# A two-layer graph network: the second layer's Q projected first and gathered into a dense table, the feed-forward's first products issued one chunk ahead

## What is computed

```
q = (x @ Wq[l].T + bq[l]) * scaling;  k = x @ Wk[l].T;  v = x @ Wv[l].T
scores = sum over a head of q[tgt] * k[srcidx]          # per edge and head
w = softmax of scores over the edges of one target
agg = segment_sum(w * v[srcidx], tgt)
x = batchnorm(x + agg @ Wo[l].T + bo[l])
x = batchnorm(x + relu(x @ W1[l].T + b1[l]) @ W2[l].T + b2[l])
```

## Time and profile before

| | us |
|---|---|
| three runs | 3073.77, 3087.56, 3089.63 |
| median | 3087.56 |
| profiled execution, span from first to last instruction | 3095.6 |
| TensorE busy in it | 2657.9 (86%) |
| VectorE, ScalarE, GpSimd busy | 1629.2, 1321.1, 1115.8 |

### The profile page before, as it was taken

The page is one execution under the profiler, slowest core; times in us unless marked ns, Lnnn a source line. Parts: engine busy times, 40 slices in busy tenths (PEclk is TensorE's granted clock), DMA queues, the critical chain, the costliest instruction groups (busy, mean ns, idle before and its releaser), DMA issues.

```text
span 3095.6 us, 78344 instructions
## 1 busy us (share of the span) xinstructions
PE 2657.9 (86%) x32605; PEld 2143.5 (69%) x32605; DVE 1629.2 (53%) x3272; ACT 1321.1 (43%) x3690; POOL 1115.8 (36%) x1130
## 2 busy tenths in 40 slices
PE   5999997999999999758899788888888678599998
PEld 4877885777777777546488577777777465477777
DVE  5236785555555555456512355555554645656553
ACT  3324443555555555422232255555555322333432
POOL 0000002666666666400001267777777111222110
PEclk8999998999999999979999899999999889799998
DMA  5642003988899998641024489999999431122211
GB/s 195 228 175 107 31 28 140 317 313 316 309 331 322 317 325 297 222 121 41 14 97 154 160 321 354 352 349 347 350 347 352 126 113 57 38 89 92 69 59 58
DMA packets 231795, 621.75 MB, mean 201 GB/s; under 512 B 39008, under 2 KB 45792, under 8 KB 231427
## 3 DMA queue, kind: packets, MB, share of 16 engines
q0 software_dynamic: 137088, 466.78, 42.2%
q1 hardware_dynamic: 94339, 149.78, 14.6%
HBM read 538.80 MB, written 103.39 MB: 207 GB/s over the span
## 4 chain that ended last, share of the span: by engine, by line
PE 60%; DMA 16%; DVE 8%; POOL 7%; issue 6%; ACT 2%; SPq 0%; DVEq 0%; POOLq 0%; ACTq 0%
PE ps L1179 6%; DMA Y<-KVd,srcE 5%; PE ps L574 5%; PE ps L575 4%; PE ps L576 4%; DMA aggd<-stage,segs 4%; PE ps L1222 4%; PE ps L1209 4%; PE ps L774 3%; POOL Y L1096 3%; PE ps L942 2%; PE ps L944 2%; PE ps L943 2%; PE ps L1186 2%; PE ps L1872 2%
## 5 line engine op out<-in xcount | busy, mean ns | idle before, releaser
L1096 POOL DMA_INDIRECT Y<-KVd,srcE x449 | 430.2, 958 | 230.6 <-issue 115.8
L1370 ACT ACTIVATE stage<-ps,stage 128x128 f32<-128x128 f32 x832 | 294.8, 366 | 115.3 <-PE ps L1186 112.4
L1096 POOL DMA_INDIRECT WA<-KVd,srcE x186 | 179.3, 964 | 361.8 <-PE ps L576 268.1
L1351 ACT ACTIVATE work<-ps 128x512 f32<-128x512 f32 x309 | 179.8, 597 | 303.8 <-PE ps L1179 303.5
L1179 PE MATMUL ps<-ident,Y 128*128 128x128 f32 x1796 | 252.2, 280 | 32.2 <-DMA Y<-KVd,srcE 26.8
L1351 ACT ACTIVATE G<-ps 128x512 f32<-128x512 f32 x315 | 181.8, 597 | 223.5 <-PE ps L1179 223.1
L1277 DVE COPY G<-ps 128x512 f32<-128x512 f32 x208 | 143.8, 691 | 245.8 <-PE ps L1186 243.0
L574 PE MATMUL ps<-Wh,xs 128*128 128x512 f32 x600 | 238.7, 398 | 31.2 <-DVE xs L514 31.2
L1179 PEld LDWEIGHTS ps<-ident,Y 128*128 128x128 f32 x1796 | 199.2, 143 | 70.5 <-issue 49.3
L575 PE MATMUL ps<-Wl,xs 128*128 128x512 f32 x600 | 236.9, 395 | 0.0
L576 PE MATMUL ps<-Wh,xs 128*128 128x512 f32 x600 | 236.5, 394 | 0.0
(11 more groups left out here) (383 smaller groups left out, 6775.2 us busy)
## 6 DMA issues: line engine op xcount, KB each, us to landing
KVd<-stage SPq DMA_DIRECT2D x96, 256.0 KB, 2.0
aggd<-work SPq DMA_DIRECT2D x6, 2048.0 KB, 7.4
Qd<-stage SPq DMA_DIRECT2D x48, 256.0 KB, 2.0
G<-aggd SPq DMA_DIRECT2D x48, 256.0 KB, 2.7
Y<-KVd,srcE POOLq DMA_INDIRECT x449
Y<-in_x SPq DMA_DIRECT2D x4, 1536.0 KB, 14.7
G<-mixq SPq DMA_DIRECT2D x24, 256.0 KB
mixd<-rowsb SPq DMA_DIRECT2D x24, 256.0 KB
```

The source lines that it names most:

```text
L1096: pool.indirect_dma_start(out=kvs[a], out_offset=None, in_=KVd[l][:, :], in_offset=bass.IndirectOffsetOnAxis(ap=srcE[:, n:n + 1], axis=0)) ...
L1351: act.activation(kT[n % len(kT)], banks(l)[place_of(l, "k", n) % len(banks(l))][:, :], ACT.Copy).then_inc(out_a, 1)
L1370: last = act.activation(pT[g % len(pT)][:, P * i:P * (i + 1)], SC[g % 2][:, P * i:P * (i + 1)], ACT.Exp, bias=smin[:, t:t + 1], scale=-1.0 ...
```

## The change

- Layer 1's projections get an order of their own: Q of all 25 tiles first, then K and V.
- While K and V are made, GpSimd gathers the query slots of all 52 pairs from `Qd` into four zeroed buffers in turn (`BOUNCE`), and SP stores each, all 128 rows, to a new DRAM table `QS`.
- In layer 1's attention SP reads a pair's slots from `QS` into `qslot`; GpSimd no longer gathers them. GpSimd's nine early fetches under Q are gone: it begins when all tables and all slots are stored. `begin1` also waits for the slots on VectorE and ScalarE. Clearing `qslot` is left out in layer 1.
- In the feed-forward of both layers the first products of chunk c+1 are issued ahead of the second products of chunk c, in two banks of their own (4 and 5); W2's four blocks use banks 0 to 3. VectorE's order is as before.
- Some semaphores are merged (`pre_in`, `flag_made` into `pre_made`, `kv_in` renamed `ring_in`).

```diff
@@ attend_pool
-            kv_stored(pool, l)
             if l == 0:
+                kv_stored(pool)
                 pool.wait_ge(qkv_mm, QKV_E)
             else:
-                pool.wait_ge(w2_mm, WO)
+                tables_stored(pool, 1)
+                begin(pool)
...
-            tables_stored(pool, l)
-            if l == 1:
-                begin(pool)
-            pool.wait_ge(filled, 7 + l)
-            fetch_slots(0)
             if l == 0:
+                tables_stored(pool, 0)
+                pool.wait_ge(filled, 7)
+                fetch_slots(0)
                 begin(pool)
             for n in range(early, early + 4):
                 fetch(n)
-            fetch_slots(1)
+            if l == 0:
+                fetch_slots(1)
...
-                if g % 2 and j < NJ:
+                if l == 0 and g % 2 and j < NJ:
                     fetch_slots(j)
...
+        def slots_sp():
+            tables_stored(sp, 1)
+            for j in range(NJ):
+                sp.wait_ge(qs_out[j % BOUNCE], 16 * (j // BOUNCE + 1))
+                if j:
+                    is_turned(sp, 1, "q", j - 1)
+                sp.dma_start(qslot, QS[P * j:P * (j + 1), :]).then_inc(slots_in, 16)
@@ finish_pe
+            def hidden(c):
+                c0, cn = CHUNKS[c]
+                is_normal(pe, 2 * l, c)
+                if c >= 2:
+                    pe.wait_ge(relu, NCK * l + c - 1)
+                for k in range(4):
+                    mm = pe.matmul(hidden_bank(c)[:, 0:cn], W1[:, k, :], xT[:, k, c0:c0 + cn], start=(k == 0), stop=(k == 3))
+                mm.then_inc(w1_mm, 1)
+
+            hidden(0)
+            pe.wait_ge(wo_add, WO * (l + 1))
             for c, (c0, cn) in enumerate(CHUNKS):
...
+                if c + 1 < NCK:
+                    hidden(c + 1)
+                pe.wait_ge(relu, NCK * l + c + 1)
+                for f in range(4):
+                    if c:
+                        pe.wait_ge(ff_add, WO * l + 4 * (c - 1) + f + 1)
+                    pe.matmul(PS[f][:, 0:cn], W2[:, f * P:(f + 1) * P], work[:, c % 3, 0:cn], start=True, stop=True
+                              ).then_inc(w2_mm, 1)
@@ second layer's projections
+        def second_qkv_pe():
+            pe.wait_ge(w_lo, 40)
+            for u in range(2 * NT):
...
+                for w in ((0,) if u < NT else (1, 2)):
...
+        def second_qkv_pool():
+            pool.wait_ge(w2_mm, WO)
+            pool.memset(gap[:, 0:512 * BOUNCE], 0.0).then_inc(filled, 1)
...
+            for j in range(NJ):
+                if j >= BOUNCE:
+                    pool.wait_ge(qs_out[j % BOUNCE], 16 * (j // BOUNCE))
+                pool.indirect_dma_start(out=bounce[j % BOUNCE], out_offset=None, in_=Qd[1][:, :],
+                                        in_offset=bass.IndirectOffsetOnAxis(ap=segs[:, j, 1:2], axis=0),
+                                        bounds_check=N - 1, oob_is_err=False).then_inc(ring_in[j % BOUNCE], 16)
+
+        def second_qkv_sp():
+            def slots_out(j):
+                sp.wait_ge(ring_in[j % BOUNCE], 16 * (uses(ET, KVN[0], j % BOUNCE) + j // BOUNCE + 1))
+                sp.dma_start(QS[P * j:P * (j + 1), :], bounce[j % BOUNCE]).then_inc(qs_out[j % BOUNCE], 16)
...
+            for v in range(2 * NT):
...
+                sp.dma_start(KVd[1][P * t:P * t + r, D * w:D * (w + 1)], stage[0:r, e % 4, :]).then_inc(st_out[e % 4], 16)
+                if v >= LAG:
+                    slots_out(v - LAG)
+            for j in range(2 * NT - LAG, NJ):
+                slots_out(j)
...
         def begin1(e):
             e.wait_ge(qkv_mm, 2 * QKV_E)
+            slots_stored(e)
```

More of the change, by code:

```diff
@@ L184, in build @@
         x_in = [sem(f"x_in{g}") for g in range(5)]
-        pre_in = [sem(f"pre_in{i}") for i in range(3)]
+        pre_in = [sem(f"pre_in{i}") for i in range(2)]
         ends_in, vec_in, nf_out = sem("ends_in"), sem("vec_in"), sem("nf_out")
@@ L697, in build @@
         snB = mt[:, 0:ET]
-        kv_in = [sem(f"kv_in{i}") for i in range(max(KVN))]
+        ring_in = [sem(f"ring_in{i}") for i in range(max(KVN))]
+        slots_in = sem("slots_in")
         q_in, sct, seg_idx = sem("q_in"), sem("sct"), sem("seg_idx")
@@ L2085, in beside_x1, with stores_before, products_by @@
                 next(later_dve, None)
-        qkv_dve(1, xs1, beside_x1)
-        qkv_act(1, xs1, x1_ready, idle, idle)
-        qkv_pe(1, xs1, Wh1, Wl1, idle)
-        qkv_sp(1, idle)
+        LAG = 2
+        bounce = [gap[:, 512 * i:512 * (i + 1)] for i in range(BOUNCE)]
+        qs_out = [sem(f"qs_out{i}") for i in range(BOUNCE)]
+        def stores_before(e):
+            return 16 * (uses(QKV_E, 4, e % 4) + e // 4)
+        def products_by(u):
+            return QKV_E + (u + 1 if u < NT else NT + 2 * (u - NT + 1))
@@ new lines, in second_qkv_dve, with low @@
+        def second_qkv_dve():
+            dve.wait_ge(row_in, ROW_Q[1])
+            dve.tensor_scalar(rowsb[:, 0, :], rowsb[:, 0, :], 0.125, None, ALU.mult).then_inc(*step_v.up())
+            def low(u):
+                t = u % NT
+                r = ROWS[t]
+                dve.wait_ge(x_hi, TURN0[1] + u + 1)
+                dve.tensor_tensor(xs1[:, u % 2, 1, :, 0:r], xT[:, :, P * t:P * t + r],
+                                  xs1[:, u % 2, 0, :, 0:r].bitcast(F32), ALU.subtract).then_inc(x_lo, 1)
+            beside_x1(0)
+            low(0)
+            dve.wait_ge(*step_v.now())
+            for t in range(NT):
+                r = ROWS[t]
+                if t + 1 < NT:
+                    beside_x1(t + 1)
+                low(t + 1)
+                dve.wait_ge(qkv_mm, QKV_E + t + 1)
+                dve.wait_ge(st_out[t % 4], stores_before(t))
+                dve.scalar_tensor_tensor(out=stage[0:r, t % 4, :], in0=PS[t % 4][0:r, :], scalar=0.125,
+                                         in1=rowsb[0:r, 0, :], op0=ALU.mult, op1=ALU.add).then_inc(q_out, 1)
+            for u in range(NT + 1, 2 * NT):
+                low(u)
@@ new lines, in second_qkv_pool @@
+        def second_qkv_pool():
+            pool.wait_ge(w2_mm, WO)
+            pool.memset(gap[:, 0:512 * BOUNCE], 0.0).then_inc(filled, 1)
+            for i in range(4):
+                pool.wait_ge(st_out[i], 16 * (uses(QKV_E, 4, i) + uses(NT, 4, i)))
+            pool.wait_ge(filled, 8)
+            for j in range(NJ):
[4 more added lines that the diff above has]
+                                        bounds_check=N - 1, oob_is_err=False).then_inc(ring_in[j % BOUNCE], 16)
@@ L2092, in build, with slots_stored @@
+        def slots_stored(e):
+            for i in range(BOUNCE):
+                e.wait_ge(qs_out[i], 16 * uses(NJ, BOUNCE, i))
+        second_qkv_dve()
+        second_qkv_act()
+        second_qkv_pe()
+        second_qkv_pool()
+        second_qkv_sp()
         area.close()
```

110 lines of the change are left out of this document (67 added, 43 removed).

## The result

The changed kernel takes 3118.24 us (median of four runs, 3102.54 to 3128.68) against 3084.45 for the kernel before beside it: a ratio of 1.0118, 95% interval 1.0086 to 1.0149. The forecast was 3083. The time lies inside the range given, 3046 to 3134, but on the side that had 27 chances in 100.

The account below looks back on a forecast made before the run. No one engine bounds the program; GpSimd sets the second attention's pace. Feed-forward +46 and attention -51 gave -5 us, carried over from the profiled execution to the 3087.56 median: 3083 us, range 3046 to 3134.

Parts of the forecast that it names:

- the side that had 27 chances in 100: Whole kernel: the chance of a slower result, 0.27, beside 0.35 for faster and 0.38 for the same.
- Bound of before: Second attention of the kernel before: GpSimd's issue sets the pair of groups, 12.80 of 12.88 us.
- Feed-forward: Both layers' feed-forward: the new order closes a loop through VectorE's normalisation, +23 us a layer, +46 in all.
- a clock loss of 1.9: Feed-forward: extra us per loop from TensorE's lower clock after idling, taken from a range of 0 to 2.5.
- the last, short chunk about level: End of each feed-forward: the last chunk was to cost about as much as before.
- Projections: Second layer's projections, Q first: slot gathers and dense stores lie under K and V; cost 0, at worst 3 us.
- Opening: Start of the second attention: K and V fetching begins near 1747.4 us, the last slot store landing about the same time.
- Attention: Steady second attention: a pair falls from 12.88 to 11.9 us, 0.43 over GpSimd's floor of 11.47; -51 us.
- three floors: Steady second attention: GpSimd 11.47, TensorE 11.14 and DMA 11.3 to 11.6 us a pair interfere with each other.
- the transfers' floor of 11.3 to 11.6 us: Steady second attention: 4.63 MB a pair at the 399 and 409 GB/s of two backlogged stretches.
- the DMA wall: Second attention: transfers stay at 350 to 355 GB/s, pairs 13.0 us, total 3138; chance 0.20.
- The overlap rival: Feed-forward: stages overlap if VectorE's additions do not hold the normalisation, 2 x -5 us, total 3027; chance 0.05.

Follow-up runs that it names:

- d4: Kernel before, with second-attention gathers after the first 25 fetching 2 KB rows instead of 4 KB; 3083.17 us in one run, pair 12.90 us.
- e3: Kernel before, with two alternating buffers for the second attention's scatter, so VectorE waits for the scatter before last; 3086.16 us in one run, pair 12.83 us.
- f2: Changed kernel with only the first four of 52 slot tables made, and read again and again; 3099.95 us in one run, first fetch at 216.3 us.
- c4: Changed kernel with six buffers instead of four into the dense table and nine fetches ahead of GpSimd's wait for it; 3112.97 us, ratio 1.0102 to before.
- d3: Changed kernel, with second-attention gathers after the first 25 fetching 2 KB rows instead of 4 KB; 3079.61 us in one run, pair 11.57 us.
- d1: Changed kernel with an extra GpSimd fill of unused memory behind every second-attention scatter; 3122.46 us, ratio 1.0132 to before, pair 12.34 us.
- best2: Changed kernel with normalisation one chunk further ahead, the opening repair and two scatter buffers; 3034.89 us, ratio 0.9864 to before, pair 12.06 us.
- d2: Changed kernel with the second attention's dense read fetching 8 of 128 rows of each slot table; 3110.50 us, ratio 1.0105 to before, pair 12.11 us.
- best: Changed kernel with normalisation one chunk further ahead, six table buffers and nine fetches ahead of GpSimd's wait; 3048.12 us, ratio 0.9889 to before, pair 12.41 us.
- c3: Changed kernel with VectorE normalising chunk c+2, not c+1, ahead of its additions of chunk c; 3060.78 us, ratio 0.9927 to before.

## Why the prediction was wrong

**Bound of before: right.** GpSimd's issue set the pair (d4: half the bytes, 12.90; e3: no wait for the last scatter, 12.83).

**Feed-forward: right mechanism, two terms too small.** The closed loop, VectorE's normalisation as releaser and the drop of the clock were there. The forecast's period was 13.15, from a clock loss of 1.9 chosen between 0 and 2.5; measured 13.70. The idle time is 4.04 us, not 4.3, yet the eight products take 6.13 us from their start to the next (1478.28 to 1484.41) where 3.43 was the pace at full clock, a loss of 2.7: the first of the three rows, set aside because the clock had dropped before its idle time, was the right measure. That is 4 x 0.55 = 2.2 us. And "the last, short chunk about level" was not: from the sixth full second products to the next stage it took 16.3 us and not 15.0, and the sixth came 0.9 later than it would have, 2.2 us again. With 0.4 at the first chunk it is 28, not 23, a layer: **+10 us in all**.

**Projections: right.** Products and stores of K and V kept their 2.72 us each beside the table.

**Opening: wrong by 9 us.** The step was "the last slot store [...] lands at about the same time". It used the landing of 2.0 us from a stretch with a DMA share of 0.30; beside the table the share is 0.69, and stores land in 3.5 and 4.1. f2 shows that the table is the cause, and c4 that most of the delay is the wait for its last slots.

**Attention: the step that failed**, and the largest: "I take 0.43 over GpSimd's floor: 11.9." Measured are 12.32, which is 0.85 over that floor: 52 x 0.42 = **22 us**. The floor itself held (11.57 in d3), and GpSimd's issue has time to spare in after (d1). The 0.43 was to pay for three floors that hold each other up, and it was chosen between two other periods, not worked out. Under it lay the transfers' floor of 11.3 to 11.6 us, from two backlogged stretches at "399 and 409 GB/s". After reaches such a rate too, 406 from 1800 to 1830 us, while GpSimd issues without a wait; over the whole steady part, in which it waits for ring places, it is 377. The forecast's objection to its own rate, that the two stretches "moved K/V gathers almost alone", is not what decides: the 30 us at 406 have dense reads and scatters among them. Nor is 377 a wall of this mix: 4.63 MB in 12.32 us is the measured period said once more, and best2 moves the same bytes at 386. What the runs do show is that the pair depends on the bytes gathered (d3) and on the dense read (d2), on the scatter's wait where best2 stands against best, and not on GpSimd's issue (d1). How these make up the 0.85 stays open.

The three add to 10 + 9 + 22 = 41; -5 and 41 make +36, against 33.8 between the medians. Of the rivals the DMA wall came nearest in time, but its sign, pairs of 12.8 us or more, did not come, and its rate of 355 or less was passed, so its 13.0 us and 3138 were too pessimistic. The Trainium skill, "DMA: Bandwidth & Descriptors", section Specifications, which that rival drew on, puts the HBM limit of a core at about 358 GB/s, as half of a stack's 716 between two cores. This program runs on one core, and over 598 us after moved 377: here the figure was no ceiling, now for longer than a few microseconds. The overlap rival failed in after; c3 made it true.

## What to carry to other kernels

When one engine's instructions are put ahead of another set, follow each value they read to the engine that makes it: if that engine makes it only after the work that was just moved behind, two stages that ran side by side become one loop, and one line in the other engine's order (here one normalisation further ahead) decides between 28 us lost and 4 gained. A rate read where transfers are backlogged gives a floor, not a forecast: after moved 406 GB/s while its gathers were issued without a wait and 377 over the long stretch in which they waited for buffers. When a bottleneck engine is relieved and several floors lie close below it, give the distance from the highest floor a range of its own: here the pair came down by 0.56 us of 12.88, and 0.85 was left over GpSimd's floor.

## What the runs showed of the hardware that was not expected

- A DMA share near 1 does not say that nothing more fits: shares of 0.97 to 1.01 went with 350 GB/s (before), 377 (after) and 386 (best2), a share of 0.74 with 215 (d3), and the time of the same packets grew when others were taken away (d2). Halving the gathered bytes at a share of 0.97 changed the pair of before by nothing that counts (12.88 and 12.90, d4).
- After 4.04 us without work the eight first products ran at the lower clock level almost to their end (granted clock 0.57, 6.2 us instead of 3.6), every time round the loop, while the gaps of 0.87 us left the clock at 1.00. A stretch of before with such gaps:

```profile
1480.00:1516.00 36.00, 32.02 (x73) 13.14 (x71) 29.14 (x47) 8.07 (x13) 0.00 (x0) 1.00 0.00 0
```
